# One-hots of nodes made by GpSimd during propagation and loaded in the slot loops of a four-layer graph network

## What is computed

```python
h = relu(layernorm(x)); x = x + propagation(h)        # 10 steps: out = spmm(out) * 0.9 + h * 0.1, then a constant
h = relu(layernorm(x)); x = x + graph_attention(h)    # tanh(softmax over a node's edges of leaky_relu(a_src[src] + a_dst[dst]), times h[src] @ W, + bias)
h = relu(layernorm(x)); x = x + dot_attention(h)      # 4 heads: exp(clip(q[src] . k[dst])) * v[dst], summed by src and divided by the weights' sum
h = relu(layernorm(x)); x = x + mean_aggregate(h)     # mean over a node's edges of h[src] @ W + b
```

## Time and profile before

| | us |
|---|---|
| median of 3 runs | 1673.04 (1671.83 to 1677.74) |
| profiled execution | 1673.17, span 1671.3 |
| build_counts | 0 to 326 |
| propagation | 326 to 857 |
| normalisation, masks and maxima | 857 to 985 |
| graph attention loop | 985 to 1202 |
| normalisation and projections | 1202 to 1241 |
| dot attention loop | 1241 to 1561 |
| normalisation | 1561 to 1602 |
| mean loop | 1602 to 1671 |

### The profile page before, as it was taken

One profiled execution on the slowest core, in us unless ns is written; L12 is line 12 of the kernel. 1 busy time (PEld: TensorE's weight loads), 2 busy tenths in 40 slices (PEclk: granted clock), 3 DMA queues, 4 the chain that ended last, 5 costly groups with the idle time before them and its releaser, 6 DMA issues. The chain is left out here.

```text
span 1671.3 us, 45748 instructions
## 1 busy us (share of the span) xinstructions
PE 1237.1 (74%) x18543; PEld 1166.1 (70%) x18544; DVE 1257.6 (75%) x2253; ACT 550.7 (33%) x1096; POOL 375.4 (22%) x208
## 2 busy tenths in 40 slices
PE   4767777499999999999952037878567777777268
PEld 3356776399999999999952027767557767767268
DVE  7888888555555555555579999999889999999712
ACT  0057777300000000000017743333356666666301
POOL 1400000000000000000000118888525555545200
PEclk6867777699999999999976559898789999999679
DMA  0012222590000000000016745555253334331583
GB/s 10 0 57 106 106 105 98 207 414 6 3 2 3 2 2 3 2 3 2 2 62 194 277 156 199 198 196 200 99 173 140 120 140 140 120 139 61 199 314 105
DMA packets 44602, 182.24 MB, mean 109 GB/s; under 512 B 14627, under 2 KB 16204, under 8 KB 43748
## 3 DMA queue, kind: packets, MB, share of 16 engines
q1 hardware_dynamic: 44052, 177.98, 29.5%
q0 software_dynamic: 336, 1.20, 0.3%
HBM read 135.03 MB, written 44.13 MB: 107 GB/s over the span
## 5 line engine op out<-in xcount | busy, mean ns | idle before, releaser
L1151 PE MATMUL psum<-work,count 128*128 128x192 f16 x6250 | 518.2, 246 | 27.5 <-issue 25.5
L1151 PEld LDWEIGHTS psum<-work,count 128*128 128x128 f16 x6250 | 516.9, 98 | 28.9 <-issue 26.4
L1090 DVE SCALAR_TENSOR_TENSOR work<-psum,small,work 128x96 f32<-128x96 f32 x250 | 79.4, 318 | 228.9 <-PE psum L1151 228.9
L1747 PE MATMUL psum<-count 128*128 128x100 f16 (+1 forms) x1875 | 187.4, 207 | 80.2 <-DVE count L1844 62.2
L1747 PEld LDWEIGHTS psum<-count 128*128 128x128 f16 x1875 | 161.9, 97 | 97.8 <-DVE count L1844 57.3
L1812 POOL TENSOR_TENSOR count<-count 128x1000 bf16<-128x1000 f32 (+1 forms) x75 | 166.7, 2223 | 159.4 <-ACT count L1796 159.4
L1481 PE MATMUL psum<-count 128*128 128x98 f16 x625 | 99.9, 211 | 135.3 <-DVE count L1528 97.8
L928 ACT ACTIVATE work<-work 128x1248 f32<-128x1248 f32 (+1 forms) x6 | 7.2, 1202 | 564.5 <-DVE work L911 564.4
L1520 POOL TENSOR_TENSOR count<-count 128x970 bf16<-128x970 f32 (+1 forms) x75 | 166.6, 2235 | 89.4 <-ACT count L1513 89.4
L1748 PE MATMUL psum<-count 128*128 128x100 f16 (+1 forms) x1875 | 186.4, 207 | 0.0
L1748 PEld LDWEIGHTS psum<-count 128*128 128x128 f16 x1875 | 165.0, 98 | 0.0
(11 more groups left out here) (284 smaller groups left out, 2739.9 us busy)
## 6 DMA issues: line engine op xcount, KB each, us to landing
count<-bucket_rows_by_dst SPq DMA_DIRECT2D x54, 800.0 KB, 4.6
count<-bucket_rows_by_src SPq DMA_DIRECT2D x54, 800.0 KB, 4.2
count_f<-count SPq DMA_DIRECT2D x5, 4000.0 KB, 31.1
count<-count_turned SPq DMA_DIRECT2D x25, 800.0 KB, 5.3
count<-count_f SPq DMA_DIRECT2D x17, 800.0 KB, 4.3
count_turned<-x SPq DMA_DIRECT2D x25, 416.0 KB, 2.4
count_turned<-x SPq DMA_DIRECT2D x25, 384.0 KB, 2.3
work<-count_f SPq DMA_DIRECT2D x8, 800.0 KB, 4.3
```

Source lines behind the costliest of these rows:

```text
L1151: last = nc.tensor.matmul(bank[i % BANKS], count16[:, j, i * P:(i + 1) * P], y[par][:, j, :], start=(j == 0), stop=(j == TILES - 1))
L1747: nc.tensor.matmul(slot(b, i, width), hot[:, t0 + i, :], high[:, of, at:at + width], start=True, stop=False, skip_group_check=True)
```

## The change

Three of the four node one-hots of a tile are no longer made in the loops: the destination one-hot of the graph loop and both of the dot loop. During propagation SyncE loads the bucket rows in halves of 1600 columns into three buffers in `x`, GpSimd compares them with the partition's number in place, and ScalarE's queue stores them to DRAM: 50 halves by destination, 100 by source. `x` is loaded behind the last store. The loops load the finished one-hots (`load_hot`), into three buffers each. In the graph loop the two-column matmuls get 98 columns, with zeros in the others, and the edge one-hot moves to the second group's turn; in the dot loop too. For further rounds a block `spot_next_round` makes the next round's one-hots; with one round in all its body and the loads for the next round are skipped by a branch. The mean stage's first block issues eight of the twelve loads, the loop the rest. Some semaphores are shared.

```diff
+class NodeSpots:
+    def loads(self, sp, halves, row, n):
+        for i in range(n):
+            if i >= 3:
+                sp.wait_ge(self.stored[i % 3], 16 * (i // 3))
+            sp.dma_start(halves[i % 3], row(i).broadcast_to([P, HALF_ROW])).then_inc(self.loaded[i % 3], 16)
+    def compares(self, pool, halves, n):
+        for i in range(n):
+            pool.wait_ge(self.loaded[i % 3], 16 * (i // 3 + 1))
+            self.nc.gpsimd.tensor_scalar(halves[i % 3], halves[i % 3], self.partition, None, ALU.is_equal).then_inc(self.spotted, 1)
+    def stores(self, act, halves, hot, n):
+        for i in range(n):
+            act.wait_ge(self.spotted, i + 1)
+            act.dma_start(hot(i), halves[i % 3]).then_inc(self.stored[i % 3], 16)
...
 def propagate
-            sp.wait_ge(x_free, 1)
-            sp.dma_start(x[:, 0:full, :], ...).then_inc(x_loaded, 16)
...
+            spots.loads(sp, halves, half_row, HALVES)
+            sp.wait_ge(x_free, 1)
+            sp.dma_start(x[:, 0:full, :], ...).then_inc(x_loaded, 16)
...
+        @block.gpsimd
+        def _(pool):
+            spots.compares(pool, halves, HALVES)
+            spots.wait_stored(pool, HALVES)
+            nc.gpsimd.memset(x[:, TILES - 1, :], 0.0).then_inc(x_free, 1)
+        @block.scalar
+        def _(act):
+            spots.stores(act, halves, half_hot, HALVES)
...
 def graph_attention
-                            nc.tensor.matmul(ps[:, at + D:at + GW], node_hot[DST][t % 2][:, s, :], bend_high[:, t, :], ...)
+                            nc.tensor.matmul(ps[:, at:at + GW], node_hot[DST][t % 3][:, s, :], wide_high[:, t, :], ...)
...
+                    if t >= 3:
+                        sp.wait_ge(S["gathered"], (t - 2) * PER)
+                        load_hot(sp, t)
...
                             if s0 == 0:
-                                spot_nodes(SRC, t + 1)
+                                spot_sources(t + 1)
                             elif s0 == GROUP:
-                                spot_nodes(DST, t + 1)
-                            else:
                                 spot_edges(t + 1)
...
-        end_round(nc, S.values())
-        first_loads(nc.sync, k + 1)
+        end_round(nc, [*S.values(), *m["spots"].all()])
+        spot_next_round(nc, m, halves, lambda i: by_dst_half(by_dst, k + 1, i), lambda i: hot_half(hot_by_dst, i), BY_DST_HALVES)
+        if_one(nc.sync, m, None, lambda: first_loads(nc.sync, k + 1))
...
 def dot_attention
+                for s in range(3, TILES):
+                    for v, done in ((SRC, "q_done"), (DST, "v_done")):
+                        sp.wait_ge(S[done], (s - 2) * PER)
+                        load_hot(sp, s, v)
...
-                            if t0 == 0:
-                                spot_nodes(SRC, s + 1)
-                            elif t0 == GROUP:
-                                spot_nodes(DST, s + 1)
-                            else:
+                            if t0 == GROUP:
                                 spot_edges(s + 1)
...
 def mean_aggregate
-        if_one(sp, m, lambda: load_first(sp))
+        if_one(sp, m, lambda: load_first(sp, 0, 2 * UNDER_WAY))
...
     def one_loads(sp):
+        load_first(sp, 2 * UNDER_WAY, READY)
```

More of the change, by code:

```diff
@@ L839, in end_round @@
     nums = sorted(k.num for k in sems)
-    assert nums == list(range(nums[0], nums[0] + len(nums)))
-    nc.gpsimd.sem_clear(range(nums[0], nums[-1] + 1))
+    for num in nums:
+        if num - 1 not in nums:
+            nc.gpsimd.sem_clear(range(num, next(n for n in range(num, num + 257) if n not in nums)))
     nc.all_engine_barrier()
@@ L932, in _, with spot_next_round, many @@
             scalar_after(act)
+def spot_next_round(nc, m, halves, row, hot, n):
+    spots = m["spots"]
+    with nc.Block() as block:
+        @block.sync
+        def _(sp):
+            if_one(sp, m, None, lambda: spots.loads(sp, halves, row, n))
+        @block.gpsimd
+        def _(pool):
+            if_one(pool, m, None, lambda: spots.compares(pool, halves, n))
+        @block.scalar
+        def _(act):
+            def many():
+                spots.stores(act, halves, hot, n)
+                spots.wait_stored(act, n)
+            if_one(act, m, None, many)
 class Residual:
@@ L1084, in propagate, with half_row, half_hot @@
     rest = Residual(nc, m, cnt_dram, "step")
+    spots, HALVES = m["spots"], BY_SRC_HALVES + BY_DST_HALVES
+    halves = [view(m["x"], i * HALF_ROW // 2, HALF_ROW, F16) for i in range(3)]
+    def half_row(i):
+        return by_dst_half(by_dst, 0, i) if i < BY_DST_HALVES else by_src_half(by_src, 0, i - BY_DST_HALVES)
+    def half_hot(i):
+        return hot_half(hot_by_dst, i) if i < BY_DST_HALVES else hot_half(hot_by_src, i - BY_DST_HALVES)
     def update(dve, n, from_bank, tile_of, y_next):
@@ L1460, in edges @@
         return v[:, 0:n * EW].rearrange("p (b i j) -> p b i j", i=PER_BANK, j=EW)
+    halves = [hot.rearrange("p t n -> p (t n)")[:, 0:HALF_ROW] for hot in node_hot[DST]]
     with nc.Fori(0, rounds_of(nc, m)) as k:
@@ L1585, in vector_end @@
     def vector_end(dve):
-        step = Count(nc, "gat_final_chain")
+        step = m["norm"].chain
         def link(ins):
```

196 lines of the change are left out of this document (110 added, 86 removed).

## The result

The changed kernel takes 2046.75 us (median of 4 runs, 2034.24 to 2054.55) against 1673.26 for the kernel before beside it: a ratio of 1.222 (95% interval 1.215 to 1.229), 373 us slower. The profiled run took 2048.42 us, with a span of 2046.6. The forecast was 1629, with a range up to 1705: wrong in sign and by 418 us.

The account below looks back on a forecast made before the run. TensorE was taken to bound propagation, while VectorE looked full in both slot loops. On 1673.17 us: graph -2, dot -46, mean stage -13, blocks +5, propagation +12, together -44, giving 1629; range 1600 to 1705.

Parts of the forecast that it names:

- The price of the comparison: Propagation: GpSimd compares 1600 elements in 1.6 us, half the slope of two-input subtractions; 3.0 if one input costs as much.
- the comparison at the two-input rate: Rival in propagation: comparison takes 3.0 us, 3.3 a half, last at 880, updates held longer; above 1710; chance 0.07.
- the first rival: Propagation: GpSimd's comparisons hold VectorE's cast and subtraction, one tile through for each; +81 for +12, so 1698; chance 0.17.
- a term of 12: Propagation: comparisons hold VectorE's updates, costing about 1.3 us at each of nine step boundaries; +12 us, bounds 0 and +35.
- The buffers' turn: Propagation: load 3.2, compare 1.6, store 2.4, hand-overs 0.5; 2.6 to 2.7 us a half, all done by 790, hidden.
- Graph loop: Graph attention's slot loop: tile falls from 8.38 to 8.30 us because the edge one-hot becomes held; -2 us, bounds -8, +8.
- The rival of the unheld edges: Graph loop: the edge one-hot is not held by GpSimd; 7.23 us a tile, 27 us less, total 1602; chance 0.12.
- Dot loop: Dot attention's slot loop: two one-hots go, saving 2.53 us a tile less 0.7 of waits; -46 us, bounds -63 and -30.
- Does it meet GpSimd there?: Dot loop: whether the moved edge one-hot meets GpSimd's subtraction behind the second group; answered that VectorE wins by 0.15 us.
- the race is lost: Rival in the dot loop: GpSimd's subtraction starts first, edges wait 1.85 us a tile; +46, total 1675; chance 0.07.
- Ahead of the mean stage: Block before the mean loop: without idle loads and with four waits, it ends with VectorE; -13 us, bounds -8, -17.
- The two blocks: Two added blocks on the path, each with a barrier, register load and jump; +5 us for both, bounds +1 and +14.

## Why the prediction was wrong, point by point

**The price of the comparison** was the step that failed first. "Half the slope, an input at a time" supposed that a form with one input can't cost more than one with two, and 3.0 us was set as the dear end. It took 4.32; over 2 us was one of the prediction's own signs of being wrong. The bound wasn't a bound, because no row showed this form; the row of another form was taken for a ceiling. The Trainium skill (GPSIMD Engine Reference, "Engine selection") says of GpSimd that "1-input is roughly line-rate"; here a one-input operation took 2.65 ns an element and a two-input one 1.78, so the trace disagrees. The 1.5 us that the prediction had from the same page was no check of the 1.6: both were under half of what was measured.

**The rival that was nearest**, the comparison at the two-input rate, had a chance of 0.07 and "above 1710". Its mechanism is what happened, at a price of 4.32 us and not 3.0: updates held still longer, and a late last comparison (at 1053 and not 880). The stage's end is later still, at 1194, because TensorE had some 68 tiles left by then. The rival was left without a worked time, and so it did not set the range. At 4.3 us the first rival's working, one tile for each comparison, gives 150 x (4.48 - 2.06) = 363 us, against 339 measured.

**The hold** itself, the first rival's mechanism, is real: 331 us of TensorE's time go away with GpSimd's comparisons. That port rule (SBUF — State Buffer, "SBUF: two separate sides" in the Trainium skill, cited in the prediction) agrees with the traces: under a GpSimd instruction of 4.3 us, 0.26 us became 3.34. For holds of 1.66 us, 3.6 us apart, the forecast's count was on the safe side (6.4 us of waits for a term of 12); at the 2.7 us that it assumed it stays untested.

**The buffers' turn** was sized at 2.6 to 2.7 us a half and is 3.6 once nothing else limits it. The terms were the load (4.6 to 4.9 us for 3.2) and the store (4.5 for 2.4): the load was scaled down from one of 800 KB that took 4.6, and the store was taken from one of 384 KB that took 2.3. Neither price held for loads and stores that run side by side; why was not tested. Had only the price of the comparison been right, the stage would still have ended 80 us late, for a term of 12; the load of `x`, which the change had put behind the last store, stood in full on the path.

**Graph loop:** forecast -2, measured +3.6; 8.30 us a tile forecast, 8.36 measured. The forecast compared with a single tile of 8.38 us, while the mean before was 8.31, so by that count 8.30 was no gain at all. The edge one-hot is held, as forecast, for 2.87 us. The rival of the unheld edges (1602) fell. The two-input VectorE instruction is held like the one-hots; no experiment was made on this loop's order.

**Dot loop:** -46 forecast, +37 measured. The step that failed is the answer to "Does it meet GpSimd there?". I compared the start of the one-hot that stood in that place before with GpSimd's start and found VectorE ahead by 0.15 us, but the edge one-hot isn't that instruction: it has a wait of its own, for the scatter of the tile before last, 0.53 us in that place. The rival "the race is lost" (0.07, +46) had the right event and little over half of the price (83 us between forecast and result). It counted the hold, and not that a hold of VectorE lets TensorE stand for 3.25 us and come back at half its clock. The rest of the sum (2.53 - 0.7 us a tile) was right: 10.8 forecast, 10.71 in the second place with a third buffer and 10.89 with the edges in the third place.

**Ahead of the mean stage** -13 forecast; -10.5 with the added block, whose 3.4 us taken off leave -13.9, and 14 us on the kernel before. **The two blocks:** +5 forecast, +4.0 and +3.4 measured (4.87 and 4.37 us of idle for 0.90 and 0.93). **Clearing on GpSimd and padding:** forecast at nothing; normalisation grew by 1.9 us, whose cause wasn't tested, and padding costs at most the 1.2 us above.

By stage, forecast and the profiled run differ by 327 us in propagation, 83 in the dot loop and 9 elsewhere.

## What to carry to other kernels

Before work goes to another engine, have a row of that very instruction form on that engine; without one, leave the dear end of the range open and work out at which price the plan turns: here at 3.1 us a half, as the prediction itself says, and both the comparison (4.3) and the transfers (3.6) lay above it. When an instruction is moved to a new place, move its own waits with it before comparing start times. And ask of a gain found on an engine that is full by busy time whether those instructions were working or only waiting for a port: taking 25 out, with the edge one-hot moved, gained nothing in the graph loop, while in the dot loop 50 less gained about 42 us once the next instruction stood in the right place.

## What the runs showed of the hardware

On GpSimd, 1600 16-bit elements cost 4.24 us with one tensor and a constant, 4.32 with a value for each partition, 2.86 with two tensors; VectorE needs 0.63 us for the comparison with a value for each partition, a seventh. A 400-element comparison took 1.28 us. Long GpSimd instructions hold short VectorE ones for most of their own length: under comparisons of 4.32 us a subtraction took 3.34 us for 0.26. At 1.28 us back to back, or 1.66 us every 3.6, five PSUM banks hid nearly all of it: TensorE waited 8.0 and 6.4 us in a whole propagation. TensorE, after standing still for 3.25 us, came back at a granted clock of 0.50 for 2.7 us. In the graph loop the granted clock was 0.97 where the two-column matmuls were padded to 98 columns and 0.87 where they were not, at the same time a tile within 0.05 us.
